# Two of eight stores per tile from GpSimd, and one leg's gates two pieces sooner, in a graph network kernel

## The reference

```
def step(h, _):
    messages = h[col] @ W_msg.T + b_msg
    agg = jax.ops.segment_sum(messages, row, num_segments=num_nodes)
    gi = agg @ W_ih.T + b_ih
    gh = h @ W_hh.T + b_hh
    r = jax.nn.sigmoid(i_r + h_r)
    z = jax.nn.sigmoid(i_z + h_z)
    n = jnp.tanh(i_n + r * h_n)
    return (1.0 - z) * n + z * h
h = step applied 5 times to x
out = layernorm(x + h)
```

## Time and profile before

| | us |
|---|---|
| median of 3 runs (lowest, highest) | 675.84 (674.34, 676.35) |
| the profiled execution | 678.04 |
| its span in the trace | 676.2 |
| PE busy | 617.7 (91%) |
| DVE busy | 335.1 (50%) |
| ACT busy | 320.0 (47%) |
| POOL busy | 260.9 (39%) |
| mean granted TensorE clock | 0.961 |

### The profile page before, as it was taken

How to read it: one execution, slowest core, us unless ns; L and a number is a source line. 1 busy time by engine, 2 the same in 40 slices (tenths; PEclk the granted TensorE clock), 3 DMA queues, 4 the chain that set the end, 5 groups by cost and what they waited for, 6 DMA issues and landing times.

```text
span 676.2 us, 8620 instructions
## 1 busy us (share of the span) xinstructions
PE 617.7 (91%) x3071; PEld 479.0 (71%) x3071; DVE 335.1 (50%) x729; ACT 320.0 (47%) x557; POOL 260.9 (39%) x349
## 2 busy tenths in 40 slices
PE   4679888888999999999899999899999989999992
PEld 4557666666755878887778878688778867788861
DVE  4799878785577223335423224532223452244456
ACT  3567677776444344444244334443344443443442
POOL 6000000000300655664456665356555436566600
PEclk9589989888999999999899999899999989999996
DMA  5134344443000000000000000000000000000012
GB/s 166 27 79 103 99 101 104 101 103 99 7 0 2 0 1 1 0 0 1 1 0 2 1 0 1 0 1 1 0 1 0 1 0 1 1 0 1 0 30 69
DMA packets 37708, 18.69 MB, mean 28 GB/s; under 512 B 4588, under 2 KB 37482, under 8 KB 37662
## 3 DMA queue, kind: packets, MB, share of 16 engines
q1 hardware_dynamic: 35304, 16.70, 9.5%
q0 software_dynamic: 416, 0.83, 0.4%
q10 hardware_dynamic: 1942, 0.55, 0.4%
HBM read 2.96 MB, written 1.60 MB: 7 GB/s over the span
## 4 chain that ended last, share of the span: by engine, by line
PE 73%; DVE 7%; DMA 6%; ACT 5%; SPq 4%; issue 3%; POOL 0%; DVEq 0%; ACTq 0%
PE PS L689 38%; PE PS L669 8%; PE PS L670 8%; PE PS L612 5%; DMA A<-stage 4%; SPq L428 4%; PE PS L677 4%; PE PS L676 4%; PE PS L532 3%; ACT spread L861 2%; PE PS L603 2%; ACT ring L907 1%; ACT stage L850 1%; DVE hT L1204 1%; DVE pre_n L1200 1%
## 5 line engine op out<-in xcount | busy, mean ns | idle before, releaser
L496 POOL CAST ring<-A 128x896 fp32r<-128x896 uint8 (+4 forms) x324 | 249.4, 806 | 376.9 <-PE PS L689 213.2
L689 PE MATMUL PS<-ring,parts 128*128 128x448 f32 x1372 | 302.9, 375 | 1.9 <-ACT ring L907 1.9
L689 PEld LDWEIGHTS PS<-ring,parts 128*128 128x128 f32 x1372 | 254.2, 188 | 32.9 <-issue 11.8
L1188 DVE SCALAR_TENSOR_TENSOR pre_n<-PS,small,gate_r 128x448 f32<-128x448 f32 x35 | 23.9, 684 | 236.0 <-PE PS L677 235.8
L907 ACT ACTIVATE ring<-A 128x896 fp32r<-128x896 uint8 (+4 forms) x144 | 106.1, 776 | 0.1
L612 PE MATMUL PS<-spread,parts 128*128 128x448 f32 x294 | 87.6, 411 | 15.2 <-ACT spread L861 15.1
L890 ACT ACTIVATE gate_r<-PS,small 128x448 f32<-128x448 f32 x35 | 22.2, 634 | 157.9 <-PE PS L670 157.9
L861 ACT ACTIVATE spread<-A 128x1056 fp32r<-128x1056 uint8 (+1 forms) x75 | 70.7, 948 | 25.5 <-DMA A<-stage 25.5
L669 PE MATMUL PS<-hT,wT 128*128 128x448 f32 x140 | 66.8, 559 | 0.6 <-ACT agg L883 0.6
L612 PEld LDWEIGHTS PS<-spread,parts 128*128 128x128 f32 x294 | 51.8, 202 | 19.1 <-issue 16.9
L1148 DVE TENSOR_TENSOR hot_key<-iota_key,keyT 128x768 bf16<-128x768 bf16 x100 | 55.5, 555 | 18.5 <-PE PS L603 16.9
(11 more groups left out here) (124 smaller groups left out, 465.8 us busy)
## 6 DMA issues: line engine op xcount, KB each, us to landing
A<-stage SPq DMA_DIRECT2D x200, 66.0 KB, 2.6
y<-in_x SPq DMA_DIRECT2D x4, 384.0 KB, 4.7
out<-y SPq DMA_DIRECT2D x4, 192.0 KB, 2.5
out<-y SPq DMA_DIRECT2D x3, 256.0 KB, 2.4
w_raw<-in_L_gnn_W_ih ACTq DMA_DIRECT2D x1, 192.0 KB, 4.2
w_raw<-in_L_gnn_W_hh ACTq DMA_DIRECT2D x1, 192.0 KB, 5.4
w_raw<-in_L_gnn_W_msg ACTq DMA_DIRECT2D x1, 64.0 KB, 2.1
bmsg<-in_L_gnn_b_msg ACTq DMA_DIRECT2D x1, 64.0 KB, 5.0
```

The lines of the kernel that those rows point to most:

```text
L496: last = nc.gpsimd.tensor_copy(to, data)
L689: mm = pe.matmul(PS[:, AGG_BANKS[(t * LEGS + b) % 2], 0:LW], parts[:, k, part, :], ring[:, SLOT_OF[at_piece] % SLOTS, k % 2, :], start=(k ...
```

## The change

Stores: the second store (side 1) of the pairs q = 0 and q = 3 of every tile is issued by POOL, on semaphores `stored_too` of their own. SP keeps six stores of a tile. All waits for a tile to land now wait for both semaphores.

Gates: in leg 6 of steps 1 to 3 the gates of leg 5 stand ahead of piece 4 instead of piece 6. DVE's and ACT's programs of that leg follow: messages 0 to 2 ahead of `before_tanh`, messages 3 to 5 between its other operations, `new_h` ahead of messages 6 and 7.

```
+STORED_TOO = (0, 3)
 GATES_AT = 6
+GATES_AT_END = 4
...
         def landed(k):
-            return 16 * GT * (k // 2 + 1)
+            return 16 * (GT - len(STORED_TOO)) * (k // 2 + 1)
+        def landed_too(k):
+            return 16 * len(STORED_TOO) * (k // 2 + 1)
+        BEFORE_GATES = 3
...  (sync)
-                    for side in range(2):
-                        ...
+                    for side in range(1 if q in STORED_TOO else 2):
+                        to, data = placing(p, side)
+                        sp.dma_start(to, data).then_inc(stored[k % 2], 16)
...  (gpsimd, before the casts)
+                for p in range(PAIRS):
+                    if p % PT in STORED_TOO:
+                        pool.wait_ge(count_kept, p + 1)
+                        nc.gpsimd.dma_start(*placing(p, 1)).then_inc(stored_too[p // PT % 2], 16)
...  (tensor, step)
-                            if b > 0 and e == GATES_AT:
+                            if b > 0 and e == (GATES_AT_END if b == LEGS - 1 and not last else GATES_AT):
...  (scalar: keep_count, spread_bytes; the same on DVE ahead of `late`)
+                        act.wait_ge(stored_too[k % 2], landed_too(k))
...  (scalar, leg)
                     if b == LEGS - 1 and not last:
-                        for u in range(5):
+                        for u in range(BEFORE_GATES):
                             high_part(t + 1, u)
...
                     if before[0]:
                         candidate(*before)
+                    if b == LEGS - 1 and not last:
+                        for u in range(BEFORE_GATES, 5):
+                            high_part(t + 1, u)
...  (vector, step, leg 6 when not last)
-                        both(t + 1, range(5))
+                        both(t + 1, range(BEFORE_GATES))
                         before_tanh(t, b - 1)
+                        message(t + 1, 3)
+                        less_cand(t, b - 1)
+                        message(t + 1, 4)
+                        low_part(t + 1, 3)
+                        times_z(t, b - 1)
                         message(t + 1, 5)
+                        low_part(t + 1, 4)
+                        new_h(t, b - 1)
                         message(t + 1, 6)
                         low_part(t + 1, 5)
-                        less_cand(t, b - 1)
                         message(t + 1, 7)
                         low_part(t + 1, 6)
-                        times_z(t, b - 1)
                         low_part(t + 1, 7)
-                        new_h(t, b - 1)
                         both(t + 1, range(EARLY, EARLY + 2))
```

More of the change, by code:

```diff
@@ L280, in gnn_kernel @@
         stored = [sem("stored0"), sem("stored1")]
+        stored_too = [sem("stored_too0"), sem("stored_too1")]
         spread_made, spread_used, late_made, late_used = (
@@ L321, in gnn_kernel, with placing @@
         PLANE_AT, LOW_AT, HIGH_AT, KEY_AT = range(4)
+        def placing(p, side):
+            k, q = divmod(p, PT)
+            row = side * P // 2 + q * GROUP
+            return (A[row:row + GROUP, k, :].rearrange("c (r w) -> c r w", r=RANGES),
+                    stage[:, p % STAGED, side % len(sides(p)), :])
         def landed(k):
-            return 16 * GT * (k // 2 + 1)
+            return 16 * (GT - len(STORED_TOO)) * (k // 2 + 1)
+        def landed_too(k):
+            return 16 * len(STORED_TOO) * (k // 2 + 1)
         SPREADS = tuple(segments(0, WIDE))
@@ L424, in _ @@
                     sp.wait_ge(count_kept, p + 1)
-                    for side in range(2):
-                        row = side * P // 2 + q * GROUP
-                        sp.dma_start(A[row:row + GROUP, k, :].rearrange("c (r w) -> c r w", r=RANGES),
-                                     stage[:, p % STAGED, side % len(sides(p)), :]).then_inc(stored[k % 2], 16)
+                    for side in range(1 if q in STORED_TOO else 2):
+                        to, data = placing(p, side)
+                        sp.dma_start(to, data).then_inc(stored[k % 2], 16)
             with sp.Else():
@@ L847, in keep_count @@
                         act.wait_ge(stored[k % 2], landed(k - 2))
+                        act.wait_ge(stored_too[k % 2], landed_too(k - 2))
                     act.wait_ge(counted, p + 1)
@@ L1173, in _ @@
                     dve.wait_ge(stored[k % 2], landed(k))
+                    dve.wait_ge(stored_too[k % 2], landed_too(k))
                     if k >= LATE:
```

## The result

| | before | after |
|---|---|---|
| median of the runs, us | 675.41 (4 runs) | 646.67 (4 runs) |
| the profiled execution, us | 678.04 | 646.73 |
| its span, us | 676.2 | 644.9 |
| mean granted clock | 0.961 | 0.978 |

The change takes 28.7 us off: ratio 0.9576, interval 0.9558 to 0.9593. Forecast were 643.2 us and -32.6; the range 638 to 659 holds the time. Between the two profiled executions the difference is 31.3 us, near the forecast. That is one of the two things to explain; the other is what each part gave.

What follows compares the result with a forecast made beforehand. SP's issue time was taken to bound the counting stage, and stalls with a slowed clock the ends of steps 1 to 3. Stores -20.9 and gates -11.7 make -32.6: 675.84 to 643.2 us, range 638 to 659.

Steps and rivals of the forecast that it cites:

- cadence, 17 tiles: Counting stage, from 62.92 us on: time per tile falls from 5.35 to 4.35 us, 17.0 us gained over 17 tiles.
- the three step ends: Ends of steps 1 to 3: each gains 3.9 us, 2.16 of stall and 1.7 of clock, together 11.7 us.
- SP's issue time as the bound: Counting stage: eight store issues of 0.671 us make 5.37 us, the tile cadence; six make 4.03, so SP stops bounding.
- That hidden 4.21 comes out: Counting stage: with SP no longer the bound, the 4.21 us per tile seen in the first stretch becomes the limit.
- 4.35 as the value: Counting stage: time taken per tile, 0.14 us over 4.21 for long issues and DMAs of two queues meeting.
- DVE as the next bound: Counting stage after the change: DVE bounds at 4.21 us per tile, with PE close to it.
- POOL's price: Counting stage: a POOL store takes 3.3 to 5.0 us from count to landed; issue time 2.6 us per tile.
- DVE undisturbed: Counting stage: POOL's stores cost DVE nothing; the upper bound was 2 x 1.01 us per tile, a cadence of 6.2.
- the terms don't depend on that: Final sum: the same 32.6 us comes off the median 675.84 as off the profiled 678.04, giving 643.2.
- POOL's landing didn't set the cadence: Counting stage rival, chance 0.15: POOL's stores need 6.5 us to land, a tile 5.1, 659 us in all.
- `new_h` wasn't late: Step-end rival, chance 0.15: POOL's casts delay `new_h`, PE stalls about 1 us or waits, 8 of 11.7 lost, 651.
- POOL kept several stores in flight: Counting stage, against the rival, chance 0.08, that POOL takes one store at a time: 7.0 us per tile, 692 in all.

Runs made afterwards that it cites:

- e7: Kernel with four stores of a tile on POOL, but DVE's high_times_value left out, output not the reference's; one execution, 645.13 us.
- e5: The whole change, but DVE and ACT keep their programs of before in leg 6, only PE's gates stand at piece 4; 665.48 us, ratio 0.9856.
- the repeated run: The kernel before, unchanged, run once more with a new profile; 677.28 us, with before's median beside it at 675.16.

## Why the prediction was right, and where it was off

| term, us | forecast | profile to profile |
|---|---|---|
| cadence, 17 tiles | 17.0 | 15.0 |
| from the last L1110 to the last count | 3.9 | 3.5 |
| around them, up to the mark | 0 | 0.6 |
| the three step ends | 11.7 | 12.2 |
| sum | 32.6 | 31.3 |

*SP's issue time as the bound:* right, shown by the series of 8, 7, 6 and 4 stores. *That hidden 4.21 comes out:* right in the tiles without a late landing. *4.35 as the value:* too low by 0.12. The term that was mis-sized is the latency of SP's own last store. The prediction has it issued about 1 us after its count and landed 2.6 later, 3.7 in all and hidden, 4.7 "just at the edge" behind a long issue. In ACT's eight waits it was 4.6 to 5.4, of which 3.3 to 4.0 is landing, and a long issue is ahead in only three of the five long tiles; five of 17 tiles took 4.8 to 5.2. By the same term two of the signs named in advance were missed: ACT's wait fell to 6.9 us and not under 5, and the last count came at 145.7 us and not near 143. *DVE as the next bound:* so it is in the first tiles, at 4.21; behind them it is PE, at 4.24 (e7). That the two lie 0.03 us apart kept this from costing anything.

*POOL's price:* between the bounds and better than the value taken: landing 3.1, issue 0.53 against 1.01, which left room for four. *DVE undisturbed:* right, `hot_row` at 498 ns. The Trainium skill (SBUF — State Buffer, "Who interferes with whom") infers that a two-input `tensor_tensor` leaves GpSimd's descriptor writing free; with DVE busy for 72.8 of 75.9 us, POOL's issues were at most 550 ns long, which agrees.

*The gates:* `before_tanh` was forecast 2.5 us sooner against the pieces and `new_h` with over 2 us to spare. Measured from the end of the last piece, `before_tanh` started 8.87 us ahead of it instead of 6.36, 2.5 sooner, and `new_h` had 2.6 to spare. e5 shows that this rests on DVE's and ACT's orders as much as on PE's.

*The step that failed* is in the sum: "the terms don't depend on that", of the profiled execution being 2.2 us above the median. They do: each fall of the clock is 1.7 us at a step's end and does not come every time, and this execution had all three. At the median the change gives 28.7, not 31.3. The 2.6 between them is the whole distance of 678.04 from 675.41. So of the 3.5 us by which the median was missed, 1.3 are the terms above and 2.2 this step. Among the 21 executions of the kernel before that ran beside the experiments one more had a clock of 0.961, and it took 678.09; the others had 0.967 to 0.980 and took 673.6 to 676.5. That the falls fill all of the 2.6 isn't shown: the repeated run had one fall less at the steps' ends, a slower counting stage, and nearly the same time.

*Rivals:* POOL's landing didn't set the cadence (SP's store was the last to land in all eight waits), `new_h` wasn't late, POOL kept several stores in flight (issues of q = 3 and the next q = 0 lie some 1.2 us apart, with 3.1 us landings).

## What to carry to other kernels

A queue that issues many small DMAs can be a stage's bound while the DMA engines are busy for 0.4 of it: multiply the issues per tile by the time from one start to the next, and compare with the cadence. Where a stage begins below that bound and slows once the queue has filled, its first tiles show the cadence that the other engines allow. When such a bound is gone, the time from the count to the landing of the last store has to be priced anew: with two queues it was longer than one queue's rows had said. When work is moved sooner on one engine, move what stands in front of its successors on the others as well, and before building a sum on one profile, check whether its slow-clock stretches belong to the kernel or to that execution.

## What the runs showed of the hardware that was not expected

- A store of 128 runs of 528 bytes costs 0.598 us of issue on SP (0.67 from start to start, with rare ones of 1.1 to 2.2) and 0.53 on POOL, whose indirect DMAs took 1.01.
- With stores from two queues in flight, SP's landings went from 2.6 to 3.3 us in the median, at a DMA share of 0.57 instead of 0.41 (two of eight stores on POOL; 2.8 with one, 3.1 with four). Whether the second queue or the denser traffic does it is not separated.
- A PE stall of 2.16 us was followed by a fall to 1.2 GHz in seven of nine cases in three profiles, and by none in two. Of e5's three stalls of 3.1 us, two were followed by one.
